# Group norm, rope and layer norms of a perceiver block on one core: fewer steps, and several of them on another engine

## The reference

```python
# 1. cross attention, 16 heads of 64, over 2048 context rows
scores = jnp.einsum('bhqd,bhkd->bhqk', q, k) * scale
attn = jax.nn.softmax(scores, axis=-1)
# 2. retention, 8 heads of 16 channels
Q, K, V = X @ W_Q, X @ W_K, X @ W_V          # per head
Q, K = _xpos(Q), _xpos(K, downscale=True)    # rope: x * c + rot(x) * s
scores = jnp.einsum('bhle,bhme->bhlm', Q, K) * D[None]   # D: decay mask
Y = jnp.einsum('bhlm,bhmv->bhlv', scores, V)
Yn = (Y - mean) * jax.lax.rsqrt(var + EPS)   # mean and var over a head's 16 channels
Yn = Yn * gn_weight + gn_bias
G = X @ W_G
out = G * jax.nn.sigmoid(G) * Yn @ W_O
# 3. four "fast feed forward" trees (q, k, v, f) of depth 8 with 256 leaves, around an attention
xn = (x - mu) / jnp.sqrt(sd + 1e-05)         # sd: deviation with ddof=1
# node decisions -> a leaf per row -> gather of that leaf's weights -> two small layers
```

## Time and profile before

| | |
|---|---|
| median of 3 runs | 719.37 us (718.36 to 719.63) |
| the profiled execution's own time | 718.43 us |
| its span | 716.2 us |
| busy: PE, DVE, ACT, POOL | 585.7, 484.1, 388.9, 280.1 us |
| granted clock of TensorE, mean | 0.937 |
| 0 to 20 us | loading, first queries |
| 20 to 600 us | the 64 heads, with the steps of batches 0 to 2 among them |
| 600 to 716 us | the tail |

### The profile page before, as it was taken

One profiled execution on the slowest core, in us unless ns is written; L12 is line 12 of the kernel. 1 busy time (PEld: TensorE's weight loads), 2 busy tenths in 40 slices (PEclk: granted clock), 3 DMA queues, 4 the chain that ended last, 5 costly groups with the idle time before them and its releaser, 6 DMA issues.

```text
span 716.2 us, 10411 instructions
## 1 busy us (share of the span) xinstructions
PE 585.7 (82%) x3950; PEld 511.7 (71%) x3950; DVE 484.1 (68%) x809; ACT 388.9 (54%) x819; POOL 280.1 (39%) x274
## 2 busy tenths in 40 slices
PE   4799999999999999798999998789999997642020
PEld 3588888988988898687878897677888986521010
DVE  2566666667776777785778777876877779333665
ACT  2465555676555556665547657665548557102420
POOL 3110002021121129751332567741514486548913
PEclk9999999999999999999999999999999999955555
DMA  9510000020000034400300171200300251034403
GB/s 222 160 45 1 1 1 1 1 60 31 30 1 1 1 118 187 122 1 1 123 1 1 63 301 33 93 1 0 122 1 2 91 216 63 1 121 166 202 0 125
DMA packets 21352, 48.51 MB, mean 68 GB/s; under 512 B 1460, under 2 KB 14648, under 8 KB 17208
## 3 DMA queue, kind: packets, MB, share of 16 engines
q0 software_dynamic: 4608, 34.74, 12.9%
q1 hardware_dynamic: 16008, 12.79, 6.4%
q10 hardware_dynamic: 688, 0.33, 0.2%
HBM read 47.59 MB, written 0.26 MB: 67 GB/s over the span
## 4 chain that ended last, share of the span: by engine, by line
PE 55%; DVE 20%; ACT 11%; POOL 6%; issue 5%; DMA 2%; POOLq 0%; ACTq 0%; DVEq 0%
PE ps_s L341 20%; PE ps_av L341 16%; PE ps_ring L494 12%; DVE chunk_max L951 7%; ACT prob L716 6%; PE ps_m L341 4%; DVE hid L813 3%; DVE pt_lo L784 3%; DVE tree L843 3%; PE ps_ring L341 3%; ACT pt_hi L744 2%; DMA leaf<-down_f_dram,idx 1%; POOL leaf L1060 1%; DVE silu L784 1%; DMA ident<-ident_in_dram 1%
## 5 line engine op out<-in xcount | busy, mean ns | idle before, releaser
L744 ACT CAST pt_hi<-ps_ring 128x512 fp32r<-128x512 f32 x256 | 144.4, 590 | 142.1 <-PE ps_ring L494 141.6
L784 DVE TENSOR_TENSOR pt_lo<-ps_ring,pt_hi 128x512 fp32r<-128x512 f32 x256 | 169.8, 685 | 64.3 <-ACT pt_hi L744 59.5
L716 ACT ACTIVATE prob<-ps_s,neg_max 128x1024 f32<-128x1024 f32 x128 | 141.6, 1114 | 53.2 <-DVE neg_max L994 53.0
L494 PE MATMUL ps_ring<-ident,prob 128*128 128x128 f32 x1024 | 145.1, 274 | 20.4 <-DVE q_lo L784 12.8
L951 DVE TENSOR_REDUCE chunk_max<-ps_s 128x1 f32<-128x1024 f32 x128 | 150.4, 1215 | 5.5 <-PE ps_s L341 5.5
L494 PEld LDWEIGHTS ps_ring<-ident,prob 128*128 128x128 f32 x1024 | 116.7, 140 | 49.2 <-issue 28.8
L341 PE MATMUL ps_av<-pt_hi,c_hi 128*128 128x256 f32 x512 | 151.0, 295 | 0.0
L341 PE MATMUL ps_av<-pt_lo,c_hi 128*128 128x256 f32 x512 | 144.7, 283 | 0.0
L341 PE MATMUL ps_av<-pt_hi,c_lo 128*128 128x256 f32 x512 | 144.7, 283 | 0.0
L341 PE MATMUL ps_s<-ct_hi,q_hi 128*128 128x512 f32 x256 | 113.5, 443 | 9.0 <-ACT prob L716 6.4
L341 PE MATMUL ps_s<-ct_hi,q_lo 128*128 128x512 f32 x256 | 102.3, 400 | 0.0
(11 more groups left out here) (235 smaller groups left out, 714.3 us busy)
## 6 DMA issues: line engine op xcount, KB each, us to landing
stage<-ctx_t_dram SPq DMA_DIRECT2D x16, 256.0 KB, 3.4
stage<-ctx_rows_dram SPq DMA_DIRECT2D x16, 256.0 KB, 2.7
leaf<-w_v_dram SPq DMA_DIRECT2D x1, 512.0 KB, 10.7
leaf<-w_o_dram SPq DMA_DIRECT2D x1, 512.0 KB, 12.1
dec<-decay_dram SPq DMA_DIRECT2D x1, 512.0 KB
nw<-node_w_dram SPq DMA_DIRECT2D x1, 510.0 KB
...
```

The lines of the kernel that those rows point to most:

```text
L494: last = nc.tensor.transpose(o[:, i * P:(i + 1) * P], prob[:, n % 2, k:k + P], ident[:])
L716: nc.scalar.activation(prob[:, n % 2, 1024 * e:1024 * (e + 1)], ps_s[:, 1024 * e:1024 * (e + 1)], ACT.Exp, bias=neg_max[:, n:n + 1], accum ...
L744: nc.scalar.copy(pt_hi[:, pp, row:row + KPC, P * (n % 2):P * (n % 2 + 1)], ps_ring[:, i % 2, :].rearrange("p (k q) -> p k q", k=KPC))\
L784: return nc.vector.tensor_tensor(o, a, b_, op)
```

## The change

- **Values centred.** The value weights have each head's mean over its 16 channels taken out once, at the start of slot 17 (`centre_values`). The products `Y` then have mean zero in each head, and `norm` needs only a sum of squares. ACT squares `Y` (`square`), DVE sums (`gsq`). The factor 16 of the mean goes into the weight (times 4) and into EPS.
- **Rope on DVE.** DVE multiplies straight out of PSUM, and ACT's copy is gone. POOL adds, and masks the queries in two halves. In batch 3 DVE also adds, and masks the first half.
- **Normalisations on DVE.** The two instructions that subtract the mean and multiply, of `xn1` and `xf`, move from POOL to DVE.
- **Scale and shift prepared.** `silu` on DVE also forms `gain` (silu times weight) and `shift` (silu times bias). After the sum of squares only one product on DVE and one product and one sum on POOL remain.
- **One power fewer.** The second layer norm and the trees' norm are one step: both factors come from the statistics of `x2`, `xl` is gone, and `root2` on POOL takes two powers and a small operation in place of three powers, a small operation and two normalisations.
- **Own banks in the last batch.** In batch 3 values and gate, the two score halves and `Y` have PSUM of their own, so PE need not wait for the reader of the bank before.
- **Places.** `norm` 48 to 49, `gate` 48 to 49, `gated_t` 49.5 to 50, `wo` 50 to 51, `x2` 51 to 52, `xf` now DVE 53; in batch 3 `vg` 43 on PE and `silu` 48.

```diff
-PE_AT = dict(of="PE", xn1_t=42, qk=43, vg=44, score0=45, score1=46, yv=47, gated_t=49.5, wo=50, xf_t=53,
+PE_AT = dict(of="PE", xn1_t=42, qk=43, vg=44, score0=45, score1=46, yv=47, gated_t=50, wo=51, xf_t=53,
...
-ACT_AT = dict(of="ACT", xn1_t=43, qk=44, vg=45, gated_t=50, xf_t=54, down0=62, down1=64, down2=66, qk_t=67,
+ACT_AT = dict(of="ACT", xn1_t=43, vg=45, square=48, gated_t=51, xf_t=54, down0=62, down1=64, down2=66, qk_t=67,
...
-DVE_AT = dict(of="DVE", x1=41, silu=45, decay0=46, decay1=47, norm=48, x2=51, xl=52, turns=55, turns_v=57, pick=56,
+DVE_AT = dict(of="DVE", x1=41, xn1=42, rope=44, silu=45, decay0=46, decay1=47, norm=49, x2=52, xf=53, turns=55, turns_v=57, pick=56,
...
-POOL_AT = dict(of="Pool", xn1=41, rope=44, mask_q=44, gate=48, xl=51, xf=52, gather_up01=56, gather_up2=58,
+POOL_AT = dict(of="Pool", root1=41, rope=44, mask_q=44, gate=49, root2=52, gather_up01=56, gather_up2=58,
...
 LAST_AT = {
-    ("PE", "logits_v"): 54, ("PE", "path_v"): 55, ("DVE", "turns_v"): 55, ("DVE", "pick_v"): 56,
+    ("PE", "vg"): 43, ("DVE", "silu"): 48, ("PE", "logits_v"): 54, ("PE", "path_v"): 55, ("DVE", "turns_v"): 55, ("DVE", "pick_v"): 56,
...
                 elif k in ("score0", "score1"):
...
+                    if b == B - 1 and not second:
+                        pe.wait_ge(S["qmask_last"], 1)
+                    else:
                         pe.wait_ge(S["qmask_ready"], b + 1)
+                    if b < B - 1 and second:
+                        pe.wait_ge(S["sm_ready"], 2 * b + 1)
...
-                elif k == "qk":
-                    act.wait_ge(S["qk_done"], b + 1)
-                    nc.scalar.copy(qk_ab[:].rearrange("p a b -> p (a b)"), m).then_inc(S["qk_copied"], 1)
...
+                elif k == "square":
+                    act.wait_ge(S["y_done"], b + 1)
+                    nc.scalar.square(ysq, y_at(b)).then_inc(S["ysq_ready"], 1)
...
+                elif k == "xn1":
+                    dve.wait_ge(S["root_ready"], 3 * b + 1)
...
+                    normalised(xn1, x_sb[:, b, :], 0).then_inc(S["xn1_ready"], 1)
+                elif k == "rope":
+                    dve.wait_ge(S["qk_done"], b + 1)
+                    roped = tt(qk_ab[:].rearrange("p a b -> p (a b)"), m, xp[:].rearrange("p a b -> p (a b)"), ALU.mult)
+                    roped.then_inc(S["roped"], 1)
+                    if b == B - 1:
+                        dve.wait_ge(S["roped"], b + 1)
+                        tt(qk_x[:], qk_a, qk_b, ALU.add).then_inc(S["qkx_ready"], 1)
+                        dve.wait_ge(S["qkx_ready"], b + 1)
+                        masked_queries(nc.vector, 0).then_inc(S["qmask_last"], 1)
                 elif k == "silu":
...
-                    tt(silu[:], gate, silu[:], ALU.mult).then_inc(S["silu_ready"], 1)
+                    link(tt(silu[:], gate, silu[:], ALU.mult))
+                    tt(gain[:], silu[:], gn[:, 0, :], ALU.mult).then_inc(S["gain_ready"], 1)
+                    dve.wait_ge(S["qmask_ready"], b + 1)
+                    tt(shift, silu[:], gn[:, 1, :], ALU.mult).then_inc(S["silu_ready"], 1)
...
                 elif k == "norm":
-                    dve.wait_ge(S["y_done"], b + 1)
-                    link(nc.vector.reduce_sum(gmean[:], groups(m[:, 0:P]), axis=AXX))
-                    link(nc.vector.tensor_scalar_mul(gmean[:], gmean[:], 1.0 / RE))
-                    bc = gmean[:].rearrange("p (h o) -> p h o", o=1).to_broadcast([P, RH, RE])
-                    link(tt(groups(yc), groups(m[:, 0:P]), bc, ALU.subtract))
-                    link(tt(ysq, yc, yc, ALU.mult))
-                    link(nc.vector.reduce_sum(gmean[:], groups(ysq), axis=AXX))
-                    nc.vector.tensor_scalar(var[:], gmean[:], 1.0 / RE, EPS, ALU.mult, ALU.add)\
-                        .then_inc(S["var_ready"], 1)
+                    dve.wait_ge(S["ysq_ready"], b + 1)
+                    link(nc.vector.reduce_sum(gsq[:], groups(ysq), axis=AXX))
+                    nc.vector.tensor_scalar_add(var[:], gsq[:], EPS * RE).then_inc(S["var_ready"], 1)
+                    dve.wait_ge(S["gain_ready"], b + 1)
+                    tt(yc, y_at(b), gain[:], ALU.mult).then_inc(S["scaled"], 1)
...
                     link(tt(x2[:], m[:, 2 * P:3 * P], x_sb[:, b, :], ALU.add))
-                    statistics(x2[:], EPS)
-                elif k == "xl":
-                    dve.wait_ge(S["xl_ready"], b + 1)
-                    statistics(xl, 0.0, scale=D / (D - 1.0))
+                    statistics(x2[:])
+                    link(nc.vector.tensor_scalar_add(var[:, 1:2], mv[:, 0, 1:2], EPS))
+                    nc.vector.scalar_tensor_tensor(var[:, 2:3], mv[:, 0, 1:2], D / (D - 1.0), var[:, 1:2], ALU.mult,
+                                                   ALU.mult).then_inc(S["var_ready"], 1)
+                elif k == "xf":
+                    dve.wait_ge(S["root_ready"], 3 * b + 3)
+                    normalised(xf[:], x2[:], 2).then_inc(S["xf_ready"], 1)
...
                 elif k == "mask_q":
                     pool.wait_ge(S["qkx_ready"], b + 1)
...
+                    if last:
+                        masked_queries(nc.gpsimd, 1).then_inc(S["qmask_ready"], 1)
+                    else:
+                        masked_queries(nc.gpsimd, 0)
+                        masked_queries(nc.gpsimd, 1).then_inc(S["qmask_ready"], 1)
...
+                elif k == "root2":
                     pool.wait_ge(S["var_ready"], variances(b, 2))
...
+                    link(root(1, 1, var[:, 2:3], 1))
+                    link(nc.gpsimd.tensor_scalar(var[:, 3:4], var[:, 1:2], EPS, rstd[:, 1:2], ALU.mult, ALU.add))
+                    root(2, 1, var[:, 3:4]).then_inc(S["root_ready"], 2)
```

More of the change, by code:

```diff
@@ L192, in program @@
         sm = qmask
-        gmean = sb("gmean", [P, RH])
-        yc, ysq = qk_a[:, 0, :], qk_a[:, 1, :]
-        gate = ysq
+        gsq = sb("gsq", [P, RH])
+        yc, ysq, gate, gated = (qk_ab[:, i, :] for i in range(4))
+        gain, shift = sb("gain", [P, D]), qk_x[:, 0, :]
         right = sb("right", [P, 3, NCH, P], BF16)
@@ L285, in variances, with vg_at, score_at, y_at @@
         def variances(b, i):
-            return 2 + 4 * b + i
+            return 2 + 3 * b + i
+        def vg_at(b):
+            return ps_s[:, 512:1024] if b == B - 1 else ps_m[:]
+        def score_at(b, second):
+            return ps_s[:, 1024 + 512 * second:1536 + 512 * second] if b == B - 1 else ps_m[:]
+        def y_at(b):
+            return ps_av[:, 0:P] if b == B - 1 else ps_m[:, 0:P]
+        def masked_queries(engine, second):
+            hs = slice(4 * second, 4 * second + 4)
+            q = qk_x[:, 0:1, :].to_broadcast([P, 4, P])
+            own_rows = hmask[:, hs].rearrange("p (h o) -> p h o", o=1).to_broadcast([P, 4, P])
+            return engine.tensor_tensor(qmask[:, hs, :], q, own_rows, ALU.mult)
         def store(sp, b):
@@ L964, in _ @@
                     tally_ways()
+                if s == BIAS_SLOT - 1:
+                    centre_values()
                 if query_pair(s - 1) is not None:
@@ L1143, in rest @@
                 last = b == B - 1
-                if k == "xn1":
+                if k == "root1":
                     pool.wait_ge(S["var_ready"], variances(b, 0))
-                    link(root(0, 1, var[:, 0:1]))
-                    if b == B - 1:
-                        pool.wait_ge(S["c_split"], CH * B)
-                    normalised(xn1, x_sb[:, b, :]).then_inc(S["xn1_ready"], 1)
-                elif k == "rope":
-                    pool.wait_ge(S["qk_copied"], b + 1)
-                    link(nc.gpsimd.tensor_tensor(qk_ab[:], qk_ab[:], xp[:], ALU.mult))
+                    root(0, 1, var[:, 0:1]).then_inc(S["root_ready"], 1)
+                elif k == "rope" and not last:
+                    pool.wait_ge(S["roped"], b + 1)
                     nc.gpsimd.tensor_tensor(qk_x[:], qk_a, qk_b, ALU.add).then_inc(S["qkx_ready"], 1)
```

83 lines of the change are left out of this document (42 added, 41 removed).

## The result

| | before | after |
|---|---|---|
| median | 719.36 us (718.36 to 719.63, 4 runs) | 726.36 us (723.64 to 726.77, 4 runs) |
| ratio, 95% interval | | 1.0085 [1.0054, 1.0115] |
| profiled execution: time, span | 718.43, 716.2 us | 723.64, 721.8 us |
| its mean granted clock | 0.937 | 0.924 |
| PE, DVE, ACT, POOL busy | 585.7, 484.1, 388.9, 280.1 us | 590.9, 491.9, 388.9, 259.4 us |

What follows compares the result with a forecast made beforehand. It took PE, busy 541.56 of 580 us at full clock, to bound the head part, and a chain of waiting operations the tail. Head +2.9 and tail -2.0 gave +0.9, so 719.3, or 720.3 us as median; range 715.6 to 724.5.

Steps and rivals of the forecast that it cites:

- `norm` moved: Head part: norm behind the maxima saves 0.93 us in batch 0 and 0.7 each in batches 1 and 2, gain 2.3.
- Rope and `xn1` in the head at no cost: Slots 21 and 22: both stand ahead of DVE's maxima, but PE's own extra products cover them, cost zero.
- Loss 2.8: Slots 38 and 54: silu's first operation waits behind POOL's up3, so PE's 1.69 us wait grows by 1.4, twice.
- `x2` and `xf`: Slots 26, 42 and 58: PE waits about 0.8 us for xf_t each time, loss 2.4, between 0 and 4.
- step 2: Tail, after the last x: vg runs first and rope, sum and mask follow on DVE; score0 comes 1.9 us sooner.
- Step 3: Tail, score0 to gated_t: score0 to norm unchanged, norm to gated_t shorter; gated_t 3.6 us sooner in all.
- 7.04 us stay: Tail, score0 to norm: the stretch keeps its length since PE was the bound, so the two banks give nothing.
- Steps 4 and 5: Tail, x2 to xf_t: the change alone leaves 3.3 us, but up3 holds xf for 4.51; xf_t 2.0 sooner overall.
- A: Rival: in the tail DVE's xf wins the race with POOL's up3, xf_t 4.2 us earlier, 716.1 us; chance 0.17.
- B: Rival: the head part does not lose, silu waits only for its two products, 717.3 us; chance 0.14.
- C: Rival: in slots 42 and 58 xf waits to the end of fold3, 2.4 us more each, 725.1 us; chance 0.14.
- D: Rival: the step that centres values or the banks does not take effect, no time of its own; chance 0.02.

Runs made afterwards that it cites:

- a_same: The changed kernel run again without an edit: 720.96 us median (716.98 to 726.06, 10 runs), ratio 1.0023 to the kernel before.
- e_before_fill: The kernel before with 66 matmuls whose results nothing reads, in PE's tail waits: 717.5 us, ratio 0.9956.
- e_after_fill: The changed kernel with 54 matmuls whose results nothing reads, in PE's tail waits: 719.27 us, ratio 0.9998.
- b_old_steps: b_both with norm, square, gate, gated_t, wo, x2, root2 and xf back at their old step numbers: 711.81 us, ratio 0.9855.
- a_silu: The changed kernel with POOL's up3 of batches 0 and 1 waiting until DVE's next silu group is done: 714.51 us, ratio 0.9911.
- a_all3: b_both with PE's xf_t moved behind the ring item of its slot (53 to 53.5): 711.5 us, ratio 0.9873.
- b_both: The changed kernel with POOL's up3 waiting for DVE's silu (batches 0 and 1) and last xf (batch 2): 710.41 us, ratio 0.9861.
- a_xf: The changed kernel with PE's xf_t moved behind the ring item of its slot (53 to 53.5): 720.97 us, ratio 1.0009.
- a_same2: The changed kernel unchanged once more, for its spread: 723.61 us median (718.52 to 725.08, 12 runs), ratio 1.0039.
- c_before_silu: The kernel before with POOL's up3 of batches 0 and 1 put behind DVE's silu: 719.5 us, ratio 0.9984.

## Why the prediction was wrong

The waits were forecast in the right places and nearly in the right sizes. The sum below compares the kernel before's trace with a_same's, both at a mean clock of 0.937. The row for the whole span holds small rests besides.

| term | forecast | measured |
|---|---|---|
| slots 20 to 27 (`norm` 0.93 off, `xf` 0.83 on) | -0.1 | -0.54 |
| slots 36 to 43 (0.7 off, 1.4 and 0.8 on) | +1.5 | +1.38 |
| slots 52 to 59 (the same) | +1.5 | +2.87, of it 1.5 half clock |
| last x to `gated_t` | -3.6 | -5.48; -4.29 at nearly full clock in both (e_before_fill, e_after_fill) |
| `gated_t` to `xf_t` (race with `up3`) | +1.6 | +1.64 |
| whole span | +0.9 | -0.2 |

- *`norm` moved.* The waits ahead of slot 24's ring item and transposes are gone, as forecast. In slot 40, 0.84 stays where it was 0.96 and 0.21, a gain of 0.33 and not 0.7. With `x2` and `xf` the move comes to nothing, as the sum of the two terms said (b_old_steps).
- *Rope and `xn1` in the head at no cost:* right. Slots 10 to 20 and 27 to 36 took the same time within 0.05.
- *`silu`.* PE's wait grew from 1.69 to 3.10 twice, the 1.4 forecast. What failed is "Loss 2.8": the wait also costs the clock behind it, 1.5 us in slot 54, and a_silu gave back 4.75 there.
- *`x2` and `xf`.* PE waited 0.61, 0.93 and 0.93 for `xf_t`, forecast 0.83, 0.8 and 0.8. But a_all3 took most of that wait away and gained only 0.06, 0.22 and 0.26, so the wait was not worth its length.
- *Tail, step 2:* `score0` 2.00 sooner after the last x in a_same, forecast 1.9. *Step 3:* last x to `gated_t` gained more than forecast. "7.04 us stay" from `score0` to `norm` was wrong in its reason. PE was not the bound by its work alone: it ran these products partly at half clock (`score0` takes 1.13 at full clock and 2.08 at half). In the changed kernel the stretch is 5.52 in a_same, with `score0` at 1.13, and 9.37 in the first trace. In the kernel before it falls from 7.04 to 5.72 with the clock kept up (e_before_fill), and in the changed kernel it is 5.52 then too (e_after_fill). So of the 7.04 some 1.3 was clock, and the banks and the new order gave 0.2. *Steps 4 and 5:* right, `xf` 4.51 beside `up3`. The Trainium skill (SBUF — State Buffer, "Who interferes with whom") has this as a lock taken by who comes first. The trace agrees: `xf` took 4.51 where `up3` started 0.07 ahead of it, and 0.34 where `up3` came behind it (b_both).
- *Rivals.* A fell: POOL won in each of the six traces with the race left in (the changed kernel's three, a_silu, a_xf, e_after_fill). B fell, since `silu` waited as forecast. C fell: PE waited 0.93 for `xf_t` in slots 42 and 58, and `fold3` did not hold `xf`. D fell: the rows of after show `yv` in a bank of its own (`ps_av`) and `norm` begin with the one sum over ACT's squares (`gsq`).

**The step that failed is the first one:** "from 20 to 600 us PE is busy for 541.56 of 580 us at full clock", read from one execution of the kernel before and carried over to the changed kernel, and with it the tail priced by rows at whatever clock they had. The sum so put the clock at no cost, without a reason. The four executions shown of the kernel before lay within 1.3 us, and I took their clock for a property of the program. In 90 further executions the kernel before gave 717.3 to 724.9, and a third of these runs had a mean clock below 0.935; the 1.4 us that the prediction took for what a measurement tells from no change was far too little. The error of 6.1 us is made up so, in executions' own times: a_same's 717.86 is 1.5 below the 719.3 of the sum; the first trace is 5.8 longer than a_same's, with 1.95 between head 63 and the last x and 4.18 between the last x and `gated_t`, both by the clock, and 0.46 given back at the start; the median of its four runs is 2.7 longer again, for which no trace stands; and 0.9 comes off, by which the forecast had already been raised to a median. The other three runs had a mean clock of 0.922, this one 0.924. A longer start would fit both numbers (its own, 105.01, is among the shortest; 3.4 us more at half clock is 0.002 of the mean), but that is an estimate and not shown. Over all 26 executions the changed kernel's median is 723.4, which lies 3.1 above the forecast and inside the range; how far off the first comparison put it was in part chance.

No rival had the clock in it. The Trainium skill (TensorE: Matmul & The Clock Gate, "HAM oscillation — how this bites in real kernels") says that waits of PE can make its clock fall and return. The trace agrees in part: the clock fell at the wait of 3.50 us in slots 38 and 54 and at that of 3.10 in slot 54, but at the 3.10 of slot 38 in one of six traces. "A longer wait of PE" was a rival with a price of its own. The runs, and no row of before, give the price: 1.5 us in slot 54, and two such prices would have put the upper end of the range near 727.5.

What stays open: why the same 3.10 wait came with half clock in slot 54 in all six traces that have it and in slot 38 in one alone (a_xf); why the clock fell in slots 62 and 63 in the first trace and a_same2 and, behind the same PE waits of 1.65 and 0.47, not in a_same; and why c_before_silu, with less waiting, ran more often at the lower clock. So the longer waits are shown as a cause of the fall in slot 54, worth 1.5 us. For the larger part, the half clock in slots 62 and 63 and in the tail, it is shown where the time went, and not what brings it there.
